# Layer norm, attention and gated ternary feed-forward on eight cores: when the first weights are asked for, and 32 extra products and a table load at launch

## The reference

```python
xn = _layernorm(x, axis=-1)
q = (xn @ Wq.T).reshape(B, T, H, hd)          # T = 2048, H = 16, hd = 64
k = (xn @ Wk.T).reshape(B, T, H, hd)
v = (xn @ Wv.T).reshape(B, T, H, hd)
attn = einsum('bqhd,bkhd->bhqk', q, k) * hd ** -0.5 * pmask   # pmask: 1 in a palace, else sigmoid(w)
s = einsum('bhqk,bkhd->bqhd', softmax(attn), v)
h = relu(xn @ quantize(W1).T + b1)            # quantize: ternary, with a threshold from mean(abs(W))
g = silu(h @ quantize(W2).T + b2)             # 1024 -> 4096 -> 1024
out = x + s * g
```

## Time and profile before

| what | value |
|---|---|
| runs of the kernel | 983.31, 987.73, 1143.85 us, median 987.73 us |
| the profiled execution, device time | 985.05 us |
| its span on the slowest core (core 5), from the first to the last instruction | 983.5 us |
| spans of the eight cores | 977.5 to 983.5 us |
| PE busy | 947.0 us, 96% of the span |
| granted TensorE clock, mean of core 5 | 0.998 |

### The profile page before, as it was taken

One profiled execution on the slowest core, in us unless ns is written; L12 is line 12 of the kernel. 1 busy time (PEld: TensorE's weight loads), 2 busy tenths in 40 slices (PEclk: granted clock), 3 DMA queues, 4 the chain that ended last, 5 costly groups with the idle time before them and its releaser, 6 DMA issues.

```text
span 983.5 us, 32845 instructions; the slowest of 8 cores (977.5 to 983.5 us)
## 1 busy us (share of the span) xinstructions
PE 947.0 (96%) x12724; PEld 388.2 (39%) x12724; DVE 695.9 (71%) x995; ACT 627.1 (64%) x739; POOL 27.4 (3%) x54
## 2 busy tenths in 40 slices
PE   2999989999999999999999999999999999999997
PEld 1443433443333333333333333333333333444443
DVE  3758878996677677767766776767676777742587
ACT  1666776776777777777777777777777776034322
POOL 0000000000000000000000000000000000100400
PEclk9999999999999999999999999999999999999999
DMA  8588787763111111121112110211110111542694
GB/s 204 153 227 263 234 274 205 227 222 102 35 45 27 41 46 45 45 46 35 33 45 45 45 46 24 45 45 46 30 49 24 45 46 44 150 117 77 185 319 161
DMA packets 30710, 100.73 MB, mean 102 GB/s; under 512 B 3680, under 2 KB 3680, under 8 KB 30304
## 3 DMA queue, kind: packets, MB, share of 16 engines
q1 hardware_dynamic: 20800, 75.56, 24.6%
q0 software_dynamic: 5152, 14.68, 7.3%
q10 hardware_dynamic: 4608, 8.39, 2.3%
HBM read 96.52 MB, written 8.39 MB: 107 GB/s over the span
## 4 chain that ended last, share of the span: by engine, by line
PE 91%; DVE 3%; issue 3%; DMA 2%; ACT 1%; DVEq 0%; ACTq 0%; POOLq 0%
PE PS L340 40%; PE PS L336 15%; PE PS L454 14%; PE PS L470 14%; PE PS L488 3%; PE PS L369 3%; PE PS L411 2%; DMA arena<-wvb 2%; ACT arena L558 1%; PE PS L392 1%; DVE arena L620 1%; DMA arena<-xP 0%; DVE arena L718 0%; PE PS L402 0%; DVE arena L720 0%
## 5 line engine op out<-in xcount | busy, mean ns | idle before, releaser
L558 ACT ACTIVATE arena<-PS 128x1024 bf16<-128x1024 f32 x512 | 498.8, 1020 | 211.3 <-PE PS L454 211.0
L340 PE MATMUL PS<-arena 128*32 128x512 bf16 x7552 | 449.8, 380 | 0.0
L340 PEld LDWEIGHTS PS<-arena 128*32 128x32 bf16 x7552 | 203.3, 97 | 204.7 <-issue 1.1
L454 PE MATMUL PS<-arena 64*128 64x512 bf16 x1024 | 160.6, 382 | 6.3 <-ACT arena L558 3.4
L470 PE MATMUL PS<-arena 128*32 128x512 bf16 x2048 | 157.6, 384 | 0.0
L336 PE MATMUL PS<-arena 128*128 128x512 bf16 x672 | 151.3, 379 | 0.0
L711 DVE TENSOR_TENSOR arena<-arena 128x1024 bf16<-128x1024 bf16 x200 | 136.3, 682 | 0.4 <-ACT arena L558 0.4
L665 DVE TENSOR_SCALAR arena<-PS,arena 128x512 bf16<-128x512 f32 x96 | 71.7, 747 | 54.6 <-PE PS L340 54.5
L700 DVE SCALAR_TENSOR_TENSOR arena<-arena 128x1024 bf16<-128x1024 f32 x64 | 82.2, 1284 | 34.4 <-PE PS L336 24.8
L336 PEld LDWEIGHTS PS<-arena 128*128 128x128 bf16 x672 | 65.6, 98 | 79.5 <-issue 0.7
L454 PEld LDWEIGHTS PS<-arena 64*128 64x128 bf16 x1024 | 32.9, 94 | 123.0 <-issue 122.6
(11 more groups left out here) (50 smaller groups left out, 428.9 us busy)
## 6 DMA issues: line engine op xcount, KB each, us to landing
arena<-w1b SPq DMA_DIRECT2D x16, 1024.0 KB, 7.4
arena<-w1b SPq DMA_DIRECT2D x32, 512.0 KB, 4.1
arena<-w2b SPq DMA_DIRECT2D x16, 1024.0 KB, 7.3
arena<-w2b SPq DMA_DIRECT2D x32, 512.0 KB, 3.9
arena<-xP SPq DMA_DIRECT2D x16, 512.0 KB, 4.5
arena<-xT POOLq DMA_DIRECT2D x32, 256.0 KB, 9.2
outT<-arena ACTq DMA_DIRECT2D x32, 256.0 KB, 4.6
arena<-wvb POOLq DMA_DIRECT2D x2, 1024.0 KB, 15.4
```

Of the source, the lines that this page charges most:

```text
L340: mm = e.matmul(out[32 * q:32 * q + 32, :], stationary[:, c * 128 + 32 * q:c * 128 + 32 * q + 32], moving[c], start=(first and c == 0), st ...
L454: mm = e.matmul(bank(b + hh), kb[hp % 2][rows, kc * 128:(kc + 1) * 128], rhs, start=True, stop=True, tile_position=(64 * hh, 0))
L558: e.activation(out=pt[gi % PR][:], in_=PS[:, b:b + 1024], func=AF.Exp, scale=0.125, bias=-4.0).then_inc(a_exp, 1)
```

## The change

V's weights are asked for at once, without the wait for the first chunk of x; K's and Q's first weights are asked for when V's have landed. The third and the fourth chunk of x are asked for when the first and the second have landed. ACT computes one ln of the constant `epsT` into `lnv[1]` at launch, before it waits for the first statistics; the result is not used. PE multiplies the identity by itself 32 times into bank 7 of PSUM as soon as the identity has landed, before the first transposes; these results are not used either.

```diff
@@ sync_program
         for tc in range(KC):
             if tc >= XR:
                 e.wait_ge(v_xh, tc - XR + 1)
+            elif tc >= 2:
+                e.wait_ge(d_x[tc - 2], 16)
             e.dma_start(out=xs[tc % XR][:], in_=xP[tc * 128:(tc + 1) * 128, :]).then_inc(d_x[tc % XR], 16)
@@ gpsimd_program
-        e.wait_ge(d_x[0], 16)
         e.dma_start(out=wv[0][:], in_=wvd[0:128, :]).then_inc(d_wv[0], 16)
+        e.wait_ge(d_wv[0], 16)
         e.dma_start(out=wk[:], in_=wkd[0:128, :]).then_inc(d_wk, 16)
         e.dma_start(out=wq[:], in_=wqd[0:128, :]).then_inc(d_wq, 16)
@@ tensor_program
         e.wait_ge(d_id, 16)
+
+        for _ in range(NWARM):
+            e.matmul(bank(7)[:, 0:128], ident[:], ident[:], start=True, stop=True)
         for tc in range(KC):
             transposes(tc)
@@ scalar_program
         e.wait_ge(v_c, 1)
+        e.activation(out=lnv[1][:], in_=epsT[:], func=AF.Ln).then_inc(a_tab, 1)
+        e.wait_ge(a_tab, 1)
         for tc in range(KC):
```

More of the change, by code:

```diff
@@ L30 @@
 TR = 4
+NWARM = 32
 NRAW = 7
@@ L261, in build_nc @@
     a_exp, a_ln, a_rc, a_u = sem("a_exp"), sem("a_ln"), sem("a_rc"), sem("a_u")
+    a_tab = sem("a_tab")
     v_c, v_sg, v_st, v_mv, v_xh = sem("v_c"), sem("v_sg"), sem("v_st"), sem("v_mv"), sem("v_xh")
```

## The result

The changed kernel is slower by a small amount: median 986.55 us (986.04 the lowest of 12 runs) beside 984.53 us for the kernel before on the same chip (982.98 the lowest), a ratio of 1.0022 with a 95% interval of 1.0012 to 1.0032. Its slowest core in the profiled execution is core 1, that of before was core 5.

What follows compares the result with a forecast made beforehand. PE, busy nearly throughout, was taken to bound the kernel, so only the start could gain: 3.8 us from the loads plus 0.5 us from the clock, 4.3 off 985.05, gave 980.8 us; range 976.5 to 985.5 us.

Steps and rivals of the forecast that it cites:

- What bounds the kernel: Whole kernel: PE is busy 947.0 of 983.5 us, so moving the start moves the end by the same amount.
- V's weights first: Launch loads: V's weights, asked for at about 0.7 us instead of 6.16, would be there by about 15 us.
- The third chunk, 14.0 us, and V's products at 17.7 us: First stage: third chunk of x lands at 14.0 us, V's products begin 3.7 us later, 3.8 us gained.
- Rows 7: Profile rows of x loads: the fifth and next two chunks took 12.7 us (median) to land behind V's weights.
- The feeders, no cost: Later x chunks and K's, Q's weights keep up with the shifted work: fifth chunk at 20 us, needed by 21.0.
- my worst case of 22.4 us: Fifth chunk's latest landing, if all of K's and Q's weights come in between; cost up to 1.4 us.
- SP's order: SP's load queue: the two new waits delay only loads wanted later or waiting anyway; cost 0.
- the table load: ACT at launch: the early ln moves a 1.28 us load that was already hidden; worth 0, bounds 0 and 0.5 us.
- The 32 products, 0.5 us: PE at launch: the identity products raise TensorE's clock for the transposes just ahead; 0.5 us gained, bounds 0 and 2.5.
- The rule of the Trainium skill: DMA queues: served packet by packet, V's products would begin at 17.0 us and the sum be 0.7 us better.
- Rival 3: Launch loads: first chunk of x lands at 13.8 us behind V's weights, V at 22.0 us; 986.5 us, chance 0.12.

Runs made afterwards that it cites:

- x1_first: The changed kernel, but SP asks for the second chunk of x ahead of the identity, at about 1.5 us; 982.87 us, ratio 0.9991.
- x1_bare: The kernel of x1_first without the 32 products and the early ln; 984.60 us, ratio 1.0002.
- kq_x4: The changed kernel, but K's and Q's first weights are asked for only when the fifth chunk of x has landed; 986.07 us, ratio 1.0010.
- launch_only: The kernel before with only the 32 products of the identity and the early ln added; 986.32 us, ratio 1.0008.
- after_again: The changed kernel once more, unaltered, on the same chip as dma_again; 986.37 us, ratio 1.0026.
- dma_again: The changed kernel without its 32 products and early ln, on the same chip as after_again; 986.39 us, ratio 1.0035.
- x_at_once: The changed kernel, but the third and fourth chunk of x are asked for at once, as before; 986.45 us, ratio 1.0012.
- warm_v: The kernel before with 64 products of the identity between the second transposes and V's first products; 986.31 us, ratio 1.0002.
- v_after_id: The changed kernel, but V's weights are asked for only when the identity has landed; 984.48 us, ratio 0.9985.
- v_after_id2: The kernel of v_after_id run once more, on the chip of x1_bare and step_warm; 983.45 us, ratio 0.9984.
- v2_step: The kernel of v_after_id with the second half of V's weights asked for one chunk later than the last chunk of x; 982.05 us, ratio 0.9983.
- step_warm: The kernel of v2_step with 48 products of the identity right before V's first products, replacing 32 at launch; 986.82 us, ratio 1.0003.

## Why the prediction was wrong

**What bounds the kernel**: right. The end moves with the start of attention; from there a core needs 911 to 914 us in both kernels.

**V's weights first**: they landed at 14.3 to 14.8 us on the eight cores, where about 15 us was taken. The landing was right, and its worth wrong.

**The third chunk, 14.0 us, and V's products at 17.7 us**: this is the step that failed. I gave the second chunk no delay of its own: I counted it among the bytes ahead of the third, and took for granted that it would be there early. But it was asked for 0.4 us behind V's weights and waited for all of them, 12.8 us. The order on DVE, which I had used for the third chunk (3.7 us from its landing), holds for every chunk: the first is normalised only when the second is there. V's start followed the second chunk, 20.51 - 14.82 = 5.7 us. But the third chunk was late as well: it landed at 16.0 to 16.4 us in the changed kernel, 16.3 in the mean, so that V's products could not have begun before 16.3 + 3.7 = 20.0 us. Of the 2.8 us by which they missed 17.7 us, about 2.3 are the third chunk's landing, and the second chunk added about 0.5. Where the second chunk was put ahead (x1_first, x1_bare), the third landed at 16.9 and 17.3 us and V's products began at about 20.8 us. So even the step as I had meant it was mis-sized, by 3 us. My upper bound for the landing, 15.0 us, divided the bytes by the mean rate of 283 KB/us; from 2 to 16 us the changed kernel's core 1 read 1.63 + 2 x 1.05 = 3.73 MB, 266 KB/us, by which the bound would have been 15.8 us. I had the third chunk land 1 us before V's weights; it landed 1.7 us after them (16.3 and 14.5 us).

**Rows 7**, by which the fifth chunk took 12.7 us to land behind V's weights, were the right rows. I used them to move the third chunk by 4 us and let them count as a rival for the first; the chunk to which they applied was the second, and that took 12.8 us.

**The feeders, no cost**: wrong. The fifth chunk was needed by 21.0 us, and its statistics began at 25.2 to 27.8 us on the eight cores, later than my worst case of 22.4 us, since it could be asked for only after the first normalise at 17.2 us, which the second chunk held up. This is where most of the loss is: idle time rose by 1.7 us. kq_x4 shows that K's and Q's weights made the fifth chunk later, and on its core 6 they made a later one late instead.

**SP's order, the table load**: for the table load nothing speaks against 0 (launch_only, and after_again beside dma_again), though it was never run apart from the 32 products. For SP's order x_at_once leaves between nothing and about 1 us.

**The 32 products, 0.5 us**: no worth in the runs (986.37 against 986.39 us with and without). The reason given was right, V's first products still took 3.4 to 3.6 us on most cores. The upper bound of 2.5 us counted two groups only: over the whole stretch the level of 1.2 GHz added 3.1 us in the mean before (3.5 on core 5). Where products did raise the clock for V's first ones, the next wait took the gain back in warm_v, and in x1_first it did not.

**The rule of the Trainium skill** that I set beside my reading ("DMA: Bandwidth & Descriptors", "Queues, rings and completion order": the engines go round their queues packet by packet) put the second chunk at 9.4 us, if both queues get half. It landed at 14.7 us. The measurement decides: equal shares are not what these queues had (81.8% and 21.8% from 4 to 12 us), and with them the forecast would have been a gain too. Whether the engines go round by packets is another question, which this does not settle.

**Rival 3** had the sign, the time and the mechanism, x behind V's weights, but put it at the first chunk, which landed at 5.4 us. I gave it 0.12.

## What to carry to other kernels

When a large load is asked for earlier, list every small load that is then asked for behind it, the next chunk and the identity too, and charge each with the large load's whole transfer, not with its share of the bytes. Then ask which of them the fixed order of the waiting engine needs first: the load that was on the critical path leaves it, and the one behind it takes its place. Asking for V's weights at launch brought V's products no sooner in any run (20.5 to 21.3 us in the mean, 20.3 before), whoever was in front. The runs whose attention began at least 0.5 us sooner than before either asked for the weights no sooner than that kernel did (v_after_id, v_after_id2, v2_step, step_warm) or had the products of the identity right ahead of V's (x1_first). What v_after_id and v2_step did was to ask for what is needed soon (here two chunks) first, then for the large load, and only then for what is needed later (the fourth chunk, K's and Q's weights). The gain is small, 1.5 to 1.7 us in 984, and only v2_step's interval lies clear of no difference.

## What the runs showed of the hardware

Half a microsecond in asking decided about 7 us in landing: on one chip the second chunk's statistics began at 14.7 to 16.0 us asked for at 1.96 us (after_again), and at 7.05 to 8.5 us asked for at about 1.5 us (x1_first), with V's weights at 1.56 us both times. The order of asking is a strong tendency and not a rule: on core 6 of step_warm the third chunk, asked for at 4.9 us and so 0.7 us before V's weights, landed at 17.4 us, where on the other seven cores it landed at 9.95 to 11.1 us. While V's weights moved (core 1 after, 4 to 12 us), x's queue had 21.8% of the engines' time and theirs 81.8%.

After an idle time TensorE was at either level: on the cores of warm_v the fourth chunk's transposes took 0.61 us (2.4 GHz) after waits of 2.30, 3.35 and 3.72 us, and 1.01 us (1.2 GHz) after waits of 2.47, 2.73 and 3.38 us; and on the cores with 3.35 and 3.72 us V's products right behind the fast transposes took 2.92 and 3.53 us, so that the slower level came after the wait and not in it. Ahead of V's first products, waits of 0 to 1.98 us behind the 64 products left them at 2.4 GHz on seven cores, and on core 3 they were at 1.2 GHz (3.57 us) after 3.15 us.
